# A graph network kernel: node work moved from passes of its own into the first edge loop

## The reference

```python
q, k, v = X @ Wq, X @ Wk, X @ Wv                     # 8 heads of 16
scores = einsum('ehd,ehd->eh', q[dst], k[src]) / 4
alpha = segment_softmax(scores, dst)
agg = segment_sum(alpha[:, :, None] * v[src], dst)
h1 = layer_norm(X + agg @ W0, ln1_g, ln1_b)
x = _layernorm(X + layer_norm(h1 + relu(h1 @ fc1 + fc1_b) @ fc2 + fc2_b, ln2_g, ln2_b))
# second layer: forward and backward edges
h = relu(concat(x[src], edge_attr, req) @ W1 + b1) @ W2 + b2
out = _layernorm(x + relu((x + segment_sum(h, dst)) @ Wu + bu))
```

## Time and profile before

| | us |
|---|---|
| median of 3 runs | 2722.23 |
| lowest and highest | 2716.83, 2722.79 |
| the profiled execution, its own time | 2717.23 |
| its span in the profile | 2715.2 |
| first loop's gathers, first start to last start | 67.6 to 1243.3 |
| second loop's gathers, first start to last start | 1491.1 to 2666.5 |

### The profile page before, as it was taken

One profiled execution on the slowest core, in us unless ns is written; L12 is line 12 of the kernel. 1 busy time (PEld: TensorE's weight loads), 2 busy tenths in 40 slices (PEclk: granted clock), 3 DMA queues, 4 the chain that ended last, 5 costly groups with the idle time before them and its releaser, 6 DMA issues.

```text
span 2715.2 us, 32144 instructions
## 1 busy us (share of the span) xinstructions
PE 1557.6 (57%) x7355; PEld 1227.2 (45%) x7356; DVE 1442.3 (53%) x2972; ACT 748.1 (28%) x1512; POOL 1592.9 (59%) x1662
## 2 busy tenths in 40 slices
PE   6354565556555555556786354556465565654656
PEld 4244455545545554455664233344343443433434
DVE  5265666666666666666575134345254353443535
ACT  3333333333433333333574011111111111111111
POOL 3665666666666666662532756665656656656661
PEclk9567767767777676767898566677677776767767
DMA  7554444444444444442011211221211212211221
GB/s 250 146 172 140 141 135 133 132 145 133 133 129 146 133 133 129 146 133 76 18 42 44 54 47 51 51 57 49 54 50 50 58 51 52 55 51 50 54 54 28
DMA packets 148256, 251.96 MB, mean 93 GB/s; under 512 B 74681, under 2 KB 99401, under 8 KB 147179
## 3 DMA queue, kind: packets, MB, share of 16 engines
q0 software_dynamic: 64048, 156.29, 20.2%
q1 hardware_dynamic: 83612, 94.45, 11.3%
q10 hardware_dynamic: 560, 0.82, 0.1%
HBM read 229.88 MB, written 21.54 MB: 93 GB/s over the span
## 4 chain that ended last, share of the span: by engine, by line
issue 29%; PE 25%; another core or an unknown queue 19%; DVE 15%; DVEq 5%; ACT 3%; DMA 2%; POOL 0%; SPq 0%; ACTq 0%; PEldq 0%; POOLq 0%
PE ps L1102 10%; PE ps L1078 8%; DVE arena L1626 4%; DVE arena L1635 2%; DVEq L1655 2%; DVE arena L1499 1%; ACT arena L880 1%; DVEq L1654 1%; PE ps L1029 1%; DMA arena<-d 1%; PE ps L1119 1%; DVEq L1652 1%; DVE arena L1445 1%; DVE arena L1554 1%
## 5 line engine op out<-in xcount | busy, mean ns | idle before, releaser
L670 POOL DMA_INDIRECT arena<-kvq_tab,arena x784 | 748.1, 954 | 455.7 <-issue 249.2
L727 POOL DMA_INDIRECT arena<-y_tab,arena x784 | 742.6, 947 | 447.5 <-issue 229.1
L1252 PEld LDWEIGHTS ps<-arena 128*128 128x128 f32 x1568 | 294.5, 255 | 407.5 <-issue 376.6
L1252 PE MATMUL ps<-arena 128*128 128x128 f32 x1568 | 319.1, 346 | 268.4 <-issue 250.9
L1102 PE MATMUL ps<-arena 128*128 128x136 f32 x1568 | 322.0, 393 | 245.7 <-issue 132.3
L1102 PEld LDWEIGHTS ps<-arena 128*128 128x128 f32 x1568 | 312.4, 297 | 268.2 <-issue 268.2
L957 ACT ACTIVATE arena<-arena 128x512 f32<-128x512 f32 x224 | 119.4, 569 | 800.1 <-DVE arena L1635 504.8
L1078 PE MATMUL ps<-arena 128*128 128x128 f32 x1596 | 286.7, 350 | 72.1 <-issue 32.3
L1239 PE MATMUL ps<-w1blk,eaT 113*128 x456 | 284.9, 709 | 64.8 <-issue 64.2
L1078 PEld LDWEIGHTS ps<-arena 128*128 128x128 f32 x1596 | 265.9, 258 | 98.4 <-issue 98.4
L1445 DVE TENSOR_TENSOR arena<-ps,arena 128x512 f32<-128x512 f32 x224 | 136.9, 611 | 320.8 <-remote 316.0
(11 more groups left out here) (258 smaller groups left out, 1973.1 us busy)
## 6 DMA issues: line engine op xcount, KB each, us to landing
arena<-d SPq DMA_DIRECT2D x59, 897.0 KB
arena<-kvq_tab,arena POOLq DMA_INDIRECT x784
arena<-y_tab,arena POOLq DMA_INDIRECT x784
kvq_tab<-arena SPq DMA_DIRECT2D x7, 1344.0 KB, 7.0
...
```

The source lines that it names most:

```text
L670: g.indirect_dma_start(kv_s[:, r, t, :], None, kvq_tab.rearrange("n (a d) -> (n a) d", a=3), bass.IndirectOffsetOnAxis(ap=v3(idx, RING)[:, ...
L727: g.indirect_dma_start(yg_s[:, r, t, :], None, y_tab, bass.IndirectOffsetOnAxis(ap=v3(idx1, RING)[:, r, t:t + 1], axis=0)).then_inc(m_g[r] ...
L1252: last = mm(bank(6 + u)[:, 0:W], yg_s[:, r, t, :], hot1_s[:, u, t, :], start=(t == 0), stop=(t == G - 1))
```

## The change

The node passes go. The first loop gets four more stages, so that nine chunks are in work: `e_` now also multiplies with W0 and adds x, `f_` does the first normalisation, `g_` fc1, relu and fc2, `h_` the second and third normalisation, and `k_` turns the result, copies it into `nodes`, multiplies for `y_tab` and stores 128 rows of it. `passes8` writes eight passes unrolled, 12 turns of four, and eight passes of drain, still 56 chunks. A chunk's window of x (64 KB) and a shifted identity (64 KB, from a small table `moves`, for the window that is cut off at the last node) are loaded in each pass; the big second load of x goes. The node buffers take the place of x in the fast memory.

Queries alternate between two PSUM banks in place of four, which leaves banks 2 and 3 to the node work. In a pass PE makes the queries of pieces 2 and 3 of the same chunk ahead of the sums and those of pieces 0 and 1 of the next chunk behind everything. POOL's wait for queries asks one chunk less. The line differences of `lanes` go from DVE to two small operations on ACT, two products on PE and the copy that L809 was. The fill of `acc1` goes to DVE at the start of the second loop. The root of the variance, a square root on ACT and a reciprocal on DVE, becomes exp(-0.5 ln(v + eps)) on ACT alone. The second loop is else as it was.

```diff
+        def passes8(eng, one_pass, n):
+
+            for c in range(LEAD):
+                one_pass(c % RING, *(c - k if c >= k else None for k in range(9)))
+            with eng.Fori(0, n) as i:
+                for c in range(RING):
+                    one_pass(c, *(i * RING + (c + LEAD - k) for k in range(9)))
+            for c in range(8):
+                one_pass(c % RING, *(n * RING + (c + LEAD - k) if k > c else None for k in range(9)))
...
+            def load_features(chunk, r):
+                base = entry0(chunk, 2, N - W)
+                sp.dma_start(v3(xw, RING)[:, r, :], x[ds(base, W), :]).then_inc(l_xw[r], 16)
+                lower = entry0(chunk, 3, W)
+                sp.dma_start(v3(sh, RING)[:, r, :], moves[ds(lower, P), :]).then_inc(l_xw[r], 16)
...
+                sp.wait_ge(n_yo, written)
+                sp.sem_inc(n_yfree, 1)
+                sp.dma_start(y_tab.rearrange("(n w) d -> n (w d)", w=2)[ds(base, W), :], v3(yst, 2)[:, u, :]).then_inc(n_yo, 16)
+                sp.reg_add(written, written, 16)
...
+                    sp.wait_ge(l_q, asked)
+                    load_queries(new + 2, u)
...
+                if new is None and a_ is not None:
+                    sp.wait_ge(s_tabi, 48)
+                    for c in range(RING):
+                        load_chunk(c, c)
...
-                if c == 3:
-                    node_rows = x.rearrange("(p t) d -> p t d", t=TILES)
-                    sp.dma_start(v3(xs[:, :], TILES)[0:NT, :, :], node_rows).then_inc(s_xr, 16)
-                    sp.dma_start(v3(xs[:, :], TILES)[NT:P, :, :], node_rows[0:P - NT, :, :]).then_inc(s_xr, 16)
...
-            asked = counter(pool, "pool_asked", BASE)
+            asked = counter(pool, "pool_asked", BASE - NP_)
...
-                if mid is None and old is None and out_ is None:
-                    g.memset(acc1, 0.0).then_inc(m_pool, 1)
-                    g.memset(deg[0:2, :], 0.0).then_inc(m_pool, 1)
...
+            def unit(at):
+
+                link(a.activation(lnv[at], mv[at][:, 1:2], ACT.Ln, bias=eps_ln[:, :]))
+                return a.activation(rstd[at], lnv[at], ACT.Exp, scale=-0.5)
+
+            def normalised(to, rows_, at):
+
+                link(unit(at))
+                link(a.activation(shift[at], neg[at], ACT.Identity, scale=rstd[at]))
+                return a.activation(to, rows_, ACT.Identity, scale=rstd[at], bias=shift[at])
+
...
+                    for j in range(2):
+                        last = a.activation(dd[:, j:j + 1], heads[:, j:j + 1], ACT.Identity, scale=-1.0, bias=heads[:, G + j:G + j + 1])
+                    last.then_inc(l_dd, 1)
...
+                if g_ is not None:
+                    a.activation(h1T, bank(3)[:, 0:W], ACT.Copy)
+                    a.activation(h1Tr, bank(3)[:, 0:W], ACT.Identity, scale=ln1_cols[:, 0:1], bias=ln1_cols[:, 2:3]).then_inc(n_hT, 1)
+                if k_ is not None:
+                    a.activation(x1T, bank(3)[:, W:2 * W], ACT.Copy).then_inc(n_xT, 1)
+                    a.activation(nodes[:, ds(base, W)], bank(3)[:, W:2 * W], ACT.Copy).then_inc(n_xn, 1)
                 if b_ is not None:
...
+                if h_ is not None:
+                    act.wait_ge(n_v2, minus7)
+                    unit(1).then_inc(n_s2, 1)
+                if new is not None or e_ is not None:
+                    act.wait_ge(n_emb, now)
+                    if e_ is not None:
+                        last = a.activation(v3(res, 2)[:, u, :], bank(7)[:, W:2 * W], ACT.Copy)
+                    if new is not None:
+                        last = a.activation(v3(paq, RING)[0:H, r, :], bank(7)[0:H, 2 * W:4 * W], ACT.Copy, scale=-BIG)
+                    last.then_inc(n_res, 1)
+                if g_ is not None:
+                    act.wait_ge(n_fcp, minus6)
+                    for c in range(FC):
+                        last = a.activation(v3(ffT, FC)[:, c, :], bank(2)[:, c * W:(c + 1) * W], ACT.Relu, bias=fc1b_all[:, c:c + 1])
+                    last.then_inc(n_f1s, 1)
+                if k_ is not None:
+                    act.wait_ge(n_yp, minus8)
+                    act.wait_ge(n_yfree, stored_)
+                    a.activation(v3(yst, 2)[:, u, :], bank(3)[:, 2 * W:4 * W], ACT.Copy).then_inc(n_ys, 1)
+                    act.reg_add(stored_, stored_, 1)
+                if f_ is not None:
+                    act.wait_ge(n_v1, minus5)
+                    normalised(h1n, v3(res, 2)[:, 1 - u, :], 0).then_inc(n_n1, 1)
                 if new is not None:
                     penalties(1 - u, (r + 1) % RING)
-                    lane_masks(new + 2, u, (r + 2) % RING)
-                for c in (minus1, minus2, minus3, minus4):
+                    lane_masks(new + 2, u)
+                if h_ is not None:
+                    act.wait_ge(n_v3, minus7)
...
-            def sqrt(k, at, norm):
-                act.wait_ge(n_v[k], at + 1)
-                a.activation(norm[2], v3(norm[1], GRP)[:, :, 1], ACT.Sqrt, bias=eps_ln[:, :]).then_inc(n_s[k], 1)
...
+                if k_ is not None and not (type(k_) is int and k_ == 0):
+                    pe.wait_ge(n_ys, minus9)
+                if g_ is not None:
+                    pe.wait_ge(n_n1, minus6)
+                    last = tp(bank(3)[:, 0:W], h1n, ident[:, :])
+                if k_ is not None:
+                    pe.wait_ge(n_x1, minus8)
+                    last = tp(bank(3)[:, W:2 * W], x1, ident[:, :])
+                if g_ is not None or k_ is not None:
+                    last.then_inc(n_hTp, 1)
+                if new is not None:
+                    queries(u, 2, True)
+                if e_ is not None:
+                    pe.wait_ge(l_avT, minus4)
+                    mm(seven[:, W:2 * W], aggT, w0_sb[:, :], start=True, stop=False)
+                    pe.wait_ge(s_init, 3)
+                    pe.wait_ge(l_xw[r], seen_x)
+                    last = mm(seven[:, W:2 * W], v3(sh, RING)[:, r, :], v3(xw, RING)[:, r, :], start=False, stop=True)
+                    if r == RING - 1:
+                        pe.reg_add(seen_x, seen_x, 32)
+                if new is not None:
+                    pe.wait_ge(l_dd, now)
+                    for j in range(2):
+                        last = mm(seven[0:H, (2 + j) * W:(3 + j) * W], dd[:, j:j + 1].to_broadcast([P, H]), ident[:, :])
+                if new is not None or e_ is not None:
+                    last.then_inc(n_emb, 1)
+                if g_ is not None:
+                    pe.wait_ge(n_hT, minus6)
+                    for c in range(FC):
+                        last = mm(bank(2)[:, c * W:(c + 1) * W], fc1_sb[:, c * P:(c + 1) * P], h1T)
+                    last.then_inc(n_fcp, 1)
+                if new is not None:
+                    queries(u, 3, True)
+                if k_ is not None:
+                    pe.wait_ge(n_xT, minus8)
+                    pe.wait_ge(n_xn, minus8)
+                    mm(bank(3)[:, 2 * W:4 * W], x1T, w1x[:, :]).then_inc(n_yp, 1)
                 if b_ is not None:
...
+                if g_ is not None:
+                    mm(six[:, 3 * W:4 * W], v3(sh, RING)[:, (r + 2) % RING, :], v3(xw, RING)[:, (r + 2) % RING, :], start=True, stop=False)
+                    mm(six[:, 3 * W:4 * W], ones[0:1, :], b2_row[0:1, :], start=False, stop=True)
+                    pe.wait_ge(n_f1s, minus6)
+                    for c in range(FC):
+                        mm(six[:, 2 * W:3 * W], v3(ffT, FC)[:, c, :], fc2_sb[:, c, :], start=(c == 0), stop=False)
+                    last = mm(six[:, 2 * W:3 * W], h1Tr, ident[:, :], start=False, stop=True)
+                if a_ is not None or c_ is not None or g_ is not None:
+                    last.then_inc(l_cd, 1)
                 if new is not None:
...
-            def lanes(r):
-                dve.wait_ge(s_init, 3)
-                dve.wait_ge(l_db, landed_l)
-                line = dstb[0:H, 0:CH].rearrange("h (p g) -> h g p", g=G)
-                more = dstb[0:H, 2:CH + 2].rearrange("h (p g) -> h g p", g=G)
-                pq_ = paq_s[0:H, r, :].rearrange("h (k p) -> h k p", k=2)
-                tt(pq_[:, 0, :], more[:, G - 2, :], line[:, 0, :], ALU.subtract)
...
-                tt(keys, v3(bank(k)[:, 0:n * D], n), keys, ALU.mult).then_inc(l_prod, 1)
+                tt(keys, v3(bank(k % 2)[:, 0:n * D], n), keys, ALU.mult).then_inc(l_prod, 1)
...
+            def moments(at, rows_):
+
+                link(v.bn_stats(stat[at], rows_), apart=True)
+                return v.bn_aggr(mv[at], stat[at])
...
+                if f_ is not None:
+                    dve.wait_ge(n_res, minus1)
+                    if not (type(f_) is int and f_ == 0):
+                        dve.wait_ge(n_n1, minus6)
+                    link(moments(0, v3(res, 2)[:, 1 - u, :]))
+                    ts(neg[0], mv[0][:, 0:1], -1.0, None, ALU.mult).then_inc(n_v1, 1)
...
+                if h_ is not None:
+                    dve.wait_ge(l_cd, minus2)
```

(15 more changed lines are left out.)

592 lines of the change are left out of this document (228 added, 364 removed).

## The result

| | us |
|---|---|
| changed kernel, median of 4 runs | 2849.84 (2848.45 to 2864.2) |
| kernel before, median of 4 runs beside it | 2719.53 (2716.22 to 2722.79) |
| ratio | 1.0491, 95% interval 1.0454 to 1.0528 |
| forecast | 2815, range 2610 to 2960 |

The account below looks back on a forecast made before the run. Prediction: POOL's gathers and stops set the first loop's period, with PE's leftover matmuls run after POOL stops. 2571.9 us outside the added period plus 48 x 5.06 gave 2815 us, range 2610 to 2960.

Parts of the forecast that it names:

- I took 26.0: First loop's steady period in us, the middle of 24.4 to 27.9, against 20.94 before; that span's chance 0.50.
- three facts that it was made from: PE results seen only after POOL stops; PE's matmuls limited per gather run; leftover matmuls, including sums, run during POOL's stop.
- 63 in a window of 15.6 us: Matmuls PE finishes in one unbroken run of gathers before crawling at 2.6 us each; the new pass has 97.
- one stop of 6 to 9 us: POOL's stand at its fifth gather in a steady pass, with sums starting only after POOL has stopped.
- the 2 us of DVE's node work ahead of the masks: Part of DVE's estimated 3 us of added work per pass, standing ahead of masks and sums, expected to hide.
- 22.1 us of work: ACT per steady pass: 14.3 us with its waits plus six table loads, 7.8 us; a floor above the old 20.94.
- rival 3: First loop: ACT and PE wait on each other, P = 30, 3007 us; with switch drains 30.3, about 3021; chance 0.13.
- Rival 1: First loop: ACT is the bound, PE not slowed by added work, P 22.1 to 23, 2628 us; chance 0.29.
- Rival 2: First loop: table loads cost nothing in effect, P stays at 20.94, 2572 us; chance 0.04.
- The balance: Change gives no more overlap than before, P within 0.1 of 23.97, no change in time; chance 0.04.
- the terms gave 114: Between loops, us: old drain 44.6, four more passes 56, fill and last store 12, last gather 1.
- the 10.9 us stall of POOL: POOL's stall at 204 to 232 us, small loads late behind the large x load; its removal counted as -11.

Follow-up runs that it names:

- e1: Changed kernel with POOL's wait for the turned ends moved ahead of the second piece instead of the fourth; ratio to the kernel before 1.117.
- e12: Kernel before with 34 PE matmuls added per first-loop pass as 17 identity products, nothing else; ratio to the kernel before 1.078.
- e3: Kernel before with POOL's wait for the sums moved ahead of the fourth piece instead of the second; ratio to the kernel before 1.046.
- e4: Changed kernel with turned-ends wait ahead of the second piece and first and third normalisation roots paired, four table loads per pass; ratio to the kernel before 1.122.
- e5: Changed kernel with POOL's wait for the turned ends ahead of the third piece instead of the fourth; 2663 us beside 2687, ratio 0.990.
- e6: Changed kernel with DVE's node work moved behind the masks and weighted values, and ACT's second-normalisation root later; ratio to the kernel before 1.033.
- e11: Changed kernel with turned-ends wait ahead of the third piece and no table loads, inverse roots not computed; ratio to the kernel before 1.011.
- e2: Changed kernel with logarithm replaced by a shift and exponential by a copy, so no table loads; ratio to the kernel before 1.034.
- e10: Changed kernel with turned-ends wait ahead of the third piece and first and third normalisation roots paired, four table loads; ratio to the kernel before 1.018.
- e7: Changed kernel with turned-ends wait ahead of the third piece and DVE's node work behind the weighted values; ratio to the kernel before 1.020.

## Why the forecast held, point by point

**The period.** I took 26.0 and it is 26.2. Of the three facts that it was made from, the first holds in nearly every pass: PE's results are seen some 2 to 3 us after POOL stops and not while it gathers on. Here and the rows of e1 say the same. The second, that PE gets only so many matmuls done in an unbroken run of gathers, is borne out by e12, e1 and e3, but not my number. I counted 63 in a window of 15.6 us. Counted over all such passes, from the start of a run to the first single matmul, the medians are 58 in the kernel before, 44 in e1, 47 in e3 and e4 and 48 in e12. What sets the number stays unknown, and in the changed kernel itself PE hardly ever reaches it. Third, I had the work that is left over fall on the sums, behind one stop of 6 to 9 us. That step failed: the sums run during a stop that I had not seen coming, and there are two, 5.9 + 3.2 us on average. The step that I left out is that POOL's wait for turned ends stands three gathers ahead of its wait for weighted values, and that DVE needs 9.7 us between the two. Moving that one wait (e5) takes 3.5 of the 5.3 us away. I cost the 2 us of DVE's node work ahead of the masks at nothing; e6 shows 1.5 us in each period for it. So the direction and the place, POOL's stops for late results, were right, but a crawl of PE that the changed kernel doesn't have was added and a DVE chain that it has was left out. That the two sizes agree to 0.2 us is luck.

**ACT.** 22.1 us of work were forecast, 20.5 are there, and the page of the profile shows its loads at the price taken. That it is a floor for the loop was never tested, as the period is 26.2; where it could have shown (e5 against e11), less work on ACT didn't help. In the drain it is the bound, and this is where the loads cost: 40 us in all (e2). The Trainium skill ("ScalarE: Activation LUTs", section "What ACT_TABLE_LOAD costs") adds a drain of about 1380 ns to each switch; in this trace L911 ends at 811.93, the load starts at 811.95 and the next activation 0.01 us behind it, so that nothing of it is to be seen, and rival 3's form with 30.3 us falls.

**The rivals.** Rival 1 (ACT as the bound, 2628) fell by its own test: POOL stops for 9.7 us in the pass shown, not under 5. Its condition, that a run of gathers sets PE no limit, was refuted by e12. Rival 2 (2572, the loads cost nothing and the period stays) fell by the period. Its first half is true in the loop, though: without the loads the period is the same (e2), and they cost 40 us in the drain alone. Rival 3 (30 us) didn't come. The balance would have needed 23.97; e5, with one wait moved, gets below it.

**Around the loop.** The node passes gave 202 us as forecast. The drain was mis-sized: 136.1 us from the last gather to the second loop's first, where the terms gave 114. I had left the old four passes at 44.6 us and added four of 14. In the trace ACT's copies into `nodes` (L885) lie 14.7, 14.8, 14.1, 14.0, 13.9, 9.5 and 8.5 us apart in the drain: all of its passes are now chains of roots on ACT, the four that were there before too. In the loop, the 10.9 us stall of POOL that I had taken off gave less: the first eight chunks take 169.6 us against 173.3, 3.7 us less. The fill on DVE, at 12 us with the last store, hides behind the gathers: the second loop takes 1173.7 us against 1175.4. Together +22 in the drain and +11 in the loop are nearly all of the 34 us between forecast and result.

**What stays open.** Why gathers hold PE's results back, and what sets the number of matmuls behind which it crawls; how the 5.3 us divide between PE's and DVE's added work in the changed kernel; why e10 and e11 settle in a slower phase than e5; how much of e7's 24.1 is ACT's chain.
